# A recommendation tower on one core: gathers without pauses, ids broadcast by DMA, one-hots compared with a column, loops written out

## The reference

```python
e = jnp.stack([tbl_0[ids[:, 0]], ..., tbl_31[ids[:, 31]]], axis=1)   # 2048 x 32 x 64
gram = jnp.einsum('bnd,bmd->bnm', e, e)
z = gram[:, rows, cols].reshape(2048, 496)                           # rows < cols
h = jnp.concatenate([z, dense_ctx], axis=1)                          # 2048 x 512
h = jnp.maximum(h @ W_top1 + b_top1, 0.0)                            # 512 -> 512
h = jnp.maximum(h @ W_top2 + b_top2, 0.0)                            # 512 -> 256
y = h @ W_top3                                                       # 256 -> 1
```

## Time and profile before

| | |
|---|---|
| median of 3 runs | 464.73 us (462.76 to 466.34) |
| the profiled execution | 465.88 us |
| its span in the profile | 464.1 us |
| PE busy | 433.8 us, 93% |
| DVE busy | 318.6 us, 69% |
| ACT busy | 202.5 us, 44% |
| POOL busy | 346.7 us, 75% |
| mean granted clock of TensorE | 0.989 |

### The profile page before, as it was taken

One profiled execution on the slowest core, in us unless ns is written; L12 is line 12 of the kernel. 1 busy time (PEld: TensorE's weight loads), 2 busy tenths in 40 slices (PEclk: granted clock), 3 DMA queues, 4 the chain that ended last, 5 costly groups with the idle time before them and its releaser, 6 DMA issues.

```text
span 464.1 us, 14700 instructions
## 1 busy us (share of the span) xinstructions
PE 433.8 (93%) x5747; PEld 382.1 (82%) x5747; DVE 318.6 (69%) x1319; ACT 202.5 (44%) x358; POOL 346.7 (75%) x490
## 2 busy tenths in 40 slices
PE   1999999999999999996999999996999999999887
PEld 0798887898799789985799789995899788998765
DVE  0789998998996488944896489853798486632300
ACT  2466745733843265322843275321753266322212
POOL 6999998988989998988989899898898992000200
PEclk9999999999999999998999999997999999999999
DMA  4445511112111211121111211131111210010010
GB/s 110 142 143 149 160 21 24 23 23 53 40 23 35 60 23 24 25 65 30 21 26 33 59 25 22 23 66 28 25 24 26 65 23 7 4 44 6 23 28 1
DMA packets 20237, 20.31 MB, mean 44 GB/s; under 512 B 9519, under 2 KB 13839, under 8 KB 20028
## 3 DMA queue, kind: packets, MB, share of 16 engines
q0 software_dynamic: 7872, 8.08, 9.9%
q1 hardware_dynamic: 12116, 11.14, 7.7%
q10 hardware_dynamic: 176, 0.08, 0.1%
HBM read 14.98 MB, written 0.08 MB: 32 GB/s over the span
## 4 chain that ended last, share of the span: by engine, by line
PE 81%; DVE 9%; issue 3%; DMA 2%; ACT 2%; SPq 2%; DVEq 0%; ACTq 0%
PE turn_ps L345 41%; PE mlp_ps L374 11%; PE gram_ps L362 8%; DVE onehot L595 6%; PE mlp_ps L384 5%; PE mlp_ps L313 5%; PE gram_ps L331 4%; PE mlp_ps L316 3%; DVE split_sb L630 2%; PE mlp_ps L398 2%; PE mlp_ps L391 2%; SPq L207 1%; DMA id_row<-half_ids 1%; PE gram_ps L398 1%; ACT h L502 1%
## 5 line engine op out<-in xcount | busy, mean ns | idle before, releaser
L595 DVE TENSOR_SCALAR onehot<-place 125x256 bf16<-125x256 f16 x1240 | 277.1, 383 | 41.5 <-PE turn_ps L345 32.8
L274 POOL DMA_INDIRECT rows<-tbl,index x240 | 234.4, 977 | 41.5 <-issue 39.0
L345 PE MATMUL turn_ps<-split_sb,onehot 125*128 125x192 bf16 x2432 | 220.5, 248 | 2.7 <-DVE split_sb L630 1.5
L345 PEld LDWEIGHTS turn_ps<-split_sb,onehot 125*128 125x128 bf16 x2432 | 199.3, 98 | 19.0 <-issue 9.7
L487 ACT CAST parts<-turn_ps 128x384 bf16<-128x384 f32 x136 | 65.1, 478 | 126.6 <-PE turn_ps L345 126.6
L281 POOL MEMSET pause<- 128x384 f32 x240 | 110.0, 458 | 0.1
L374 PE MATMUL mlp_ps<-pairs,w_sb 128*128 128x256 f32 x256 | 56.9, 381 | 1.0 <-DMA pairs<-dense 1.0
L374 PEld LDWEIGHTS mlp_ps<-pairs,w_sb 128*128 128x128 f32 x256 | 48.0, 190 | 7.8 <-DMA pairs<-dense 1.5
L576 DVE COPY y_room<-mlp_ps 1x256 f32 (+1 forms) x8 | 5.0, 627 | 65.7 <-PE mlp_ps L391 65.7
L495 ACT ACTIVATE place<-gram_ps,shift_sb 125x1024 f16<-125x1024 f32 (+1 forms) x45 | 44.3, 987 | 3.3 <-PE gram_ps L331 2.9
L459 ACT COPY emb_t<-mlp_ps 128x512 f32<-128x512 f32 x58 | 33.9, 585 | 23.8 <-PE mlp_ps L313 22.9
(11 more groups left out here) (38 smaller groups left out, 172.0 us busy)
## 6 DMA issues: line engine op xcount, KB each, us to landing
pairs<-folded SPq DMA_DIRECT2D x122, 32.0 KB
rows<-tbl,index POOLq DMA_INDIRECT x240, 2.5
emb_t<-tbl SPq DMA_DIRECT2D x8, 250.0 KB
folded<-tbl SPq DMA_DIRECT2D x5, 312.5 KB
w_sb<-w SPq DMA_DIRECT2D x1, 1024.0 KB
y_room<-tbl SPq DMA_DIRECT2D x3, 312.5 KB
w_sb<-w SPq DMA_DIRECT2D x1, 512.0 KB
pairs<-dense SPq DMA_DIRECT2D x32, 4.0 KB
```

Of the source, the lines that this page charges most:

```text
L274: nc.gpsimd.indirect_dma_start(rows[:, s % 2, slot - UNITS, t, :], None, tables[f][:, :], bass.IndirectOffsetOnAxis(index[:, s, t, f:f + 1 ...
L345: last = nc.tensor.matmul(turn_ps[:, u % 2].rearrange("p k b -> p (k b)")[:, t * PARTS * DIM:(t + 1) * PARTS * DIM], onehot[:, u % RING, c ...
L595: last = nc.vector.tensor_scalar(onehot[:, u % RING, c, :], place[:, parity, u, :], float(c), None, ALU.is_equal)
```

## The change

- GpSimd's pauses go: the gathers follow one another, held only by the waits for the halves of `rows`.
- `place` holds the ids themselves, and the compare takes its constant from a column: `codes_sb` has, for each span, one column for every c with span x partition + c in each partition.
- For supers 2 to 7 `place` is filled by one transfer from `ids_scratch` to all 125 partitions (`refill_place`), issued by SP ahead of the pairs' transfers of the same step, once the one-hots of super s - 2, which used this half of `place`, have been made. Spreads and placing copies remain in the head, for supers 0 and 1, with other pieces: 4, 4, 4, 4 and 1 units.
- Unit 16's lookup moves from slot 4 to slot 7, between layer 2 and layer 3. The ring and the result banks are now counted through all supers, so the one-hots of the next super no longer wait for all lookups of this one.
- The hardware loops are written out on every engine.
- `WARM_FIRST` goes from 40 to 12, `WARM_NEXT` from 10 to 4.

```diff
-WARM_FIRST, WARM_NEXT, WARM_LAST = 40, 10, 32
+WARM_FIRST, WARM_NEXT, WARM_LAST = 12, 4, 32
...
-PIECES = [(0, 4), (4, 8), (8, 9), (9, 13), (13, 17)]
+PIECES = [(0, 4), (4, 8), (8, 12), (12, 16), (16, 17)]
...
-GRAM_UNITS = [[7, 8], [9, 10], [11, 12], [13, 14], [15, 16]]
+GRAM_UNITS = [[7, 8], [9, 10], [11, 12], [13, 14], [15], [], [], [16]]
...
-            def refill_id_row(s, of):
-
-                sp.wait_ge(ids_spread, len(PIECES) * s)
-                sp.dma_start(id_row[:], scratch.ap()[bass.ds(of, 1)].rearrange("s u q -> s (u q)")).then_inc(id_row_loaded, 16)
+            def refill_place(s, parity):
+
+                sp.wait_ge(onehot_ready, UNITS * (s - 1))
+                sp.dma_start(place[:, parity], scratch.ap()[s:s + 1].to_broadcast([TP, UNITS, SUPER])
+                             ).then_inc(place_loaded[parity], 16)
...
+            for s in range(SUPERS - 1):
+                if s + 2 < SUPERS:
+                    refill_place(s + 2, s % 2)
+                rearrange_pairs(s, s % 2)
             rearrange_pairs(SUPERS - 1, 1, own=SP_MOVES)
...
-                        before = next(pauses)
-                        if before:
-                            pool.wait_ge(paused, before)
-                        nc.gpsimd.memset(pause[:], 0.0).then_inc(paused, 1)
...
-                n = u if first else UNITS * s - (UNITS - FIRST_UNITS) + u
-                if first or u >= FIRST_UNITS:
+                n = UNITS * s + u
+                if first:
                     pe.wait_ge(table_split, u + 1)
-                if u >= 2:
+                if n >= 2:
                     pe.wait_ge(looked_up, n - 1)
...
                     transpose_group(s, parity, turn, g, 2 if ahead else 4)
-                    if ahead and g in SPREAD_IN_TURN:
-                        spread_ids(s + 2, SPREAD_IN_TURN[g])
...
-            with pe.Fori(0, SUPERS // 2 - 1) as pair:
+            for pair in range(SUPERS // 2 - 1):
                 step(2 * pair + 1, 1, pair)
                 step(2 * pair + 2, 0, pair + 1)
...
-                nc.scalar.activation(place[:, parity, a:b, :].rearrange("p u q -> p (u q)"),
-                                     gram_flat[0:TP, piece % 2, 0:SUPER * (b - a)], ACT.Identity,
-                                     bias=shift_sb[:, piece:piece + 1]).then_inc(placed, 1)
+                nc.scalar.copy(place[:, s, a:b, :].rearrange("p u q -> p (u q)"),
+                               gram_flat[0:TP, piece % 2, 0:SUPER * (b - a)]).then_inc(placed, 1)
...
-                if first or u == 0:
+                if first or s == 1 and u == 0:
                     dve.wait_ge(placed, len(PIECES) * s + (PIECE_OF[u] + 1 if first else len(PIECES)))
-                if not first or u >= RING:
-                    dve.wait_ge(lookup_ready, UNITS * s + (u - RING + 1 if u else 0))
+                elif u == 0:
+                    dve.wait_ge(place_loaded[parity], 16 * (s // 2))
+                n = UNITS * s + u
+                if n >= RING:
+                    dve.wait_ge(lookup_ready, n - RING + 1)
                 for c in range(SPAN[u]):
-                    last = nc.vector.tensor_scalar(onehot[:, u % RING, c, :], place[:, parity, u, :],
-                                                   float(c), None, ALU.is_equal)
+                    last = nc.vector.tensor_scalar(onehot[:, n % RING, c, :], place[:, parity, u, :],
+                                                   codes_sb[:, CODE_AT[SPAN[u]] + c:CODE_AT[SPAN[u]] + c + 1], None, ALU.is_equal)
```

More of the change, by code:

```diff
@@ L1 @@
 from contextlib import ExitStack
-from itertools import count
 import numpy as np
@@ L45 @@
 RING = 4
[L47 removed]
+PIECES = [(0, 4), (4, 8), (8, 12), (12, 16), (16, 17)]
 PIECE_OF = [p for p, (a, b) in enumerate(PIECES) for _ in range(a, b)]
[L49 to L50 removed]
+assert len(PIECE_OF) == UNITS == FIRST_UNITS
+SPANS = sorted(set(SPAN))
+CODE_AT = {span: sum(SPANS[:n]) for n, span in enumerate(SPANS)}
 SPREAD_FIRST_NEXT = {8 + piece: piece for piece in range(len(PIECES))}
 TURN_UNITS = [[]] + [[u] for u in range(GROUPS - 1)]
[L54 removed]
+GRAM_UNITS = [[7, 8], [9, 10], [11, 12], [13, 14], [15], [], [], [16]]
 assert [u for units in TURN_UNITS + GRAM_UNITS for u in units] == list(range(UNITS))
[L56 removed]
+assert len(GRAM_UNITS) == SLOTS
 READY_MADE = 3
[L58 removed]
+assert READY_MADE < RING and READY_MADE <= UNITS
 SP_MOVES = 10
[L60 removed]
 MOVES = [(i, jq) for i in range(QUAD) for jq in range(QUAD)]
@@ L92, in slot_meaning, with build @@
     return rows, np.tile(second, (QUAD, SIDE))
-def build(nc, ids, tables, dense, w1, b1, w2, b2, w3, identity, second, looked_ids, shift, out):
+def build(nc, ids, tables, dense, w1, b1, w2, b2, w3, identity, second, looked_ids, codes, out):
     fp32, i32, bf16, fp16 = mybir.dt.float32, mybir.dt.int32, mybir.dt.bfloat16, mybir.dt.float16
@@ L265, in _ @@
         def _(pool):
-            pauses = count()
             def gather(s, begin=UNITS):
@@ L558, in _ @@
             act.wait_ge(weights_loaded, 16 * WEIGHTS)
-            with act.Fori(0, SUPERS // 2 - 1) as pair:
+            for pair in range(SUPERS // 2 - 1):
                 step(2 * pair + 1, 1)
@@ L643, in _ @@
             step(0, 0, mlp=False)
-            with dve.Fori(0, SUPERS // 2 - 1) as pair:
+            for pair in range(SUPERS // 2 - 1):
                 step(2 * pair + 1, 1)
@@ L680 @@
                        .reshape(P, UNITS * BATCH // P))
-    shift = given("shift", np.stack([-SPAN[a] * np.arange(TP) for a, _ in PIECES], axis=1).astype(np.float32))
+    codes = given("codes", np.concatenate([span * np.arange(TP)[:, None] + np.arange(span) for span in SPANS], axis=1)
+                  .astype(np.float32))
     out = nc.dram_tensor("out", (BATCH, 1), mybir.dt.float32, kind="ExternalOutput").ap()
-    build(nc, ids, tables, dense, w1, b1, w2, b2, w3, identity, second, looked_ids, shift, out)
+    build(nc, ids, tables, dense, w1, b1, w2, b2, w3, identity, second, looked_ids, codes, out)
     return run_bass_kernel_spmd(nc, [arrays], core_ids=[0]).results[0]["out"]
```

65 lines of the change are left out of this document (24 added, 41 removed).

## The result

The changed kernel takes 422.90 us (median of 4 runs, 422.19 to 423.48), the kernel before 465.53 (4 runs, 462.76 to 469.74): ratio 0.910, interval 0.905 to 0.915. The profiled execution took 422.19 us, 43.7 less than that of before.

What follows compares the result with a forecast made beforehand. TensorE (PE) was taken to bound the steps, VectorE the head. Savings of 20.8 + 10.3 + 4.2 + 5.2 = 40.5 us took the profiled 465.88 to 425.4; forecast 424 us, as the median is 1.15 lower, range 414 to 442.

Steps and rivals of the forecast that it cites:

- Spreads: PE's products that copy ids over partitions leave steps 0 to 6: 2.97 us a step, 20.8 us saved.
- Loops: Two loop returns behind layer 3, with the slow clock after each, vanish in straight-line code: 10.3 us saved.
- Rival (c): The written-out program stalls as the loop did, at new places or in the fetch: 434 us; chance 0.04.
- Lookup between layers: Unit 16's lookup fills PE's wait before layer 3, 0.70 us in each of steps 1 to 6: 4.2 us saved.
- Head: Fewer warm-up products let VectorE go on 3.2 us sooner, quiet time behind gathers gives 2 us: 5.2 us saved.
- Rival (d): PE's clock stays low in the head and PE sets the pace there: 429 to 434 us; chance 0.05.
- A gather alone holds VectorE 0.40 us: GpSimd's gather, without its pause, costs VectorE's one-hots 0.40 us, taken from a possible 0.13 to 0.60 us.
- The column costs nothing: VectorE's compare reading its constant from a column adds 0 ns a one-hot; the step's margin bears 42 ns.
- the tight stretch: From layer 3's release of VectorE to unit 15's lookup: PE needs 32 us, VectorE 27 us for 118 one-hots and more.
- the margin of 5 us: VectorE's spare time between layer 3's release and unit 15's lookup, 27 us of 32, so PE stays the bound.
- Rival (b): The column makes one-hots dearer and VectorE the bound: 430 to 458 us, chance 0.08; slower than before, 0.05.
- The pause's removal is worth nothing in the steps: Dropping GpSimd's pause between gathers saves nothing in the steps, since PE stays the bound there: 0 us.

Runs made afterwards that it cites:

- unrolled_again: The kernel before with its loops written out as straight-line code, nothing else changed: 454.27 us, ratio 0.976.
- experiment 4: Two parts alone on the kernel before: loops written out, 454.27 us (0.976); spreads, placing copies and row transfers left out of the steps, 448.59 us (0.967).
- imm_pause: The changed kernel with the immediate constant in the compare and GpSimd's pause both back: 425.56 us, ratio 0.913 to the kernel before.
- unit16_back: The changed kernel with unit 16's lookup back in slot 4: 698.80 us on a chip where the kernel before takes 564.19.
- unit16_again: The changed kernel with unit 16's lookup back in slot 4, once more: 698.35 us on a chip where the kernel before takes 566.73.

## Why the prediction came out

The forecast of 424 us was 1.1 us off by the medians; the profiled execution lost 43.7 us where the sum had 40.5. Of the 3.2 us between them 1.0 is in the tail, for which the sum had nothing, about 1.7 in steps 0 and 1 (3.60 and 4.72 us gained, 2.97 and 3.67 forecast) and 1.1 in steps 2 to 5 (26.1 gained, 25.0 forecast with the loops); the head gave 0.6 less. Term by term:

- **Spreads, 20.8 us: right.** From unrolled_again to the changed kernel a step falls from 49.54 to 45.91, by 3.63 us, for spread and moved lookup together (2.97 + 0.70 = 3.67 forecast); less the 0.63 of the lookup that leaves 3.0 us a step. What I didn't see: alone, on the kernel before, this edit brings only 15 of them, since VectorE has no room for a shorter step 0 (by my reading in experiment 4, as long as it starts late into it and the pauses stay). With the rest of the change, even with the pause left in (imm_pause), steps 0 and 1 fall by 2.8 and 3.9 us from unrolled_again's. The place transfer is hidden, as said: no wait for it in any step.
- **Loops, 10.3 us: right**, 11.1 measured alone (9.4 to 12.7). Rival (c) did not come: the longer program cost nothing on the chips of that kind. On the two others PE has long idle time labelled issue, but beside gathers and not by the program's length: the kernel before, with its loops, takes 564 us there, and writing them out gained 18 (0.967).
- **Lookup between layers, 4.2 us: right in kind**, 0.63 us a step, 3.8 in six.
- **Head, 5.2 us: the sum right, its parts not.** Step 0 begins 4.6 us sooner. By the heads of the four kernels that is 1.9 us for the short warm-up with the new pieces of ids, beside the pause (72.06 to 70.13), 8.45 for the pause taken out (to 61.68), less 5.75 for the column (to 67.43), where I had 3.2 for the warm-up and 2 for quiet time behind the gathers. The short warm-up is worth more, 4.7 us, once the pause is out. Rival (d) did not come: the granted clock is 1.00 from 15.00 to 67.00 us.
- **A gather alone holds VectorE 0.40 us: wrong.** This is the step that failed, in the split of 0.60 us between gather and pause. I split by duration; it measured 0.13 and 0.47, the end of my range that I had set aside.
- **The column costs nothing: wrong**, 61 ns, above the 42 that I had named as the point where the steps suffer. But that point rested on the 0.40. With both errors the tight stretch needs 118 x 0.205 + 2.9 = 27.1 us (205 ns is a column one-hot beside gathers), where I had 27; with the column's price and my gather it would have been 118 x 0.202 + 2.9 + 7.6 = 34.3 of 32, over 2 us too long in each step. The two errors cancelled, and the margin of 5 us was there by luck. Rival (b) was right in its premise and wrong in its price to the steps; it does take its 6 us in the head.
- **The pause's removal is worth nothing in the steps: right for immediate constants** in steps 2 to 5 (45.98 and 45.95 us; in steps 0 and 1 it gives the 0.9 us each that I had left in), wrong for the column, where it is worth 2.7 us in each of steps 2 to 5 and 35.8 in all. The two edits belong together, and the prediction weighed them one by one.
- The period of gathers without pause is 1.25 us, not 1.14: the gap ahead of each grew from 0.16 to 0.30 us. No row shows that it changed the time.

## What to carry to other kernels

When two edits meet at one engine, measure all four combinations: here each price on its own was mis-sized, and one mixed pair (column with pause) costs 36 us. Split a joint cost by measuring one of its parts alone, not in proportion to durations. And a stretch without PE waits on one chip is no proof for another: the edit that helps here (no pause between gathers) made the kernel before 158 us slower on one where PE all but stops beside unbroken gathers, so such a change wants runs on several chips.

## What was not expected of the hardware

- A memset of 128x384 on GpSimd held VectorE's compare for 0.43 to 0.47 us of its 0.47, in the immediate and in the column form; an indirect gather of 0.95 us held it for 0.13 and for 0.1 or less.
- The same compare of 125x256, fp16 to bf16, takes 139 ns with an immediate constant and 200 with a column of one value per partition.
- On two of six chips kernels without pauses took 698 to 722 us. PE's products then began only at multiples of some 0.70 us while gathers ran back to back (in unit16_back, on the other of the two, single ones each 1.40 us); in unit16_again 44 products in 36 us, against 543 in 38 on another chip.
- Without a memset between them, gathers follow each other with 0.30 us of issue in place of 0.16.
